# A two-layer recurrent kernel on one core: the small part of the output projection run as two half-height products side by side

## The chip, the cores and the metric

The kernel runs on one core of one Trainium2 chip. The metric is the device time of one execution in microseconds, the median over the executions that were timed. Lower is better.

## The reference: what is computed

The input `x` has 128 rows (batch), 128 time steps and 512 features; `cond` has 128 rows of 512. Two layers are added to `x` one after the other. The first is a state-space layer: a convolution over time and a projection give a gate pair `B_t`, `C_t` of 64 numbers each, `u = x @ Ws` gives 64 numbers, a state decays and accumulates, and its read-out `y` (64 numbers a step) is projected back to 512 features by `Wo`. The second is a plain recurrent layer with a 512 by 512 matrix. Cut to what matters:

```python
def step(state, inputs):
    u_t, b_t, c_t = inputs
    state = decay * state + dt * b_t * u_t
    return (state, c_t * state)
...
return y @ Wo + bo
...
def step(h, xw_t):
    h_next = jnp.tanh(h @ Wh + xw_t)
    return (h_next, h_next)
...
x = x + _L0_cond_ref(x, cond_1024[:, None, :], ...)
x = x + _L1_cond_ref(x, cond_1024, ...)
```

## The kernel before, in words

**Precision by splitting.** Most products are taken in the float32r type. An operand is split into a high part (the value rounded to float32r) and a low part (the rest), and a product is made of several: high by high, high by low, low by high. Names end in `_hi` and `_lo` for the parts. `y_hl` holds both parts of `y` in one tile of 128 rows: the low part of the 64 numbers in rows 0 to 63 (`0:N`), the high part in rows 64 to 127 (`N:P`). `wo_hi` and `wo_lo` hold the scaled `Wo` twice, once in each half of the rows, so that one product of `wo_hi` (128 rows) with `y_hl` sums high and low `y` at once.

**Stages.** The first 311 us or so hold the convolution, the transposes and the projection (lines 705 to 716 and 768 to 789). Then a loop over 32 groups of four time steps runs (`steps`, lines 791 to 818 for TensorE, with a body of the same shape on ScalarE, VectorE and GpSimd). Two groups are written out ahead, a hardware loop covers the middle, and the last ones are written out behind. In group g the recurrence of the second layer runs its four steps, and in the gaps the first layer of group g+1 is computed.

**One step on TensorE** is: `z_first` of the next step (8 products of 512 columns, lines 746 and 747), four transposes of the new `h` (line 801), `z_second` (4 products, line 753) and `z_recur` (12 products, lines 761, 762, 765). Beside that, step 0 holds `u_second` (4 products, line 728), step 3 holds `u_first` (4 products, line 722) ahead of its `z_second`, and step 2 holds `wo_product` (lines 731 to 738) between `z_second` and `z_recur`: for each of four chunks c of 128 output features, `wo_hi` by `y_hl` (line 736) and `wo_lo` by `y_hl` (line 737) are summed in one PSUM bank.

**The chain from wo_product to the next group.** When a chunk's bank is done (`wo_done`), VectorE adds it to `x` (`x1_sum`, line 591, chunks 0 and 1 right after line 633, then line 636, then chunks 2 and 3). ScalarE rounds the sum to the high part `x1_hi` (`x1_copy`, line 433), GpSimd subtracts for the low part `x1_lo` (`x1_rest`, line 354), chunk by chunk in order. TensorE's `z_first(0)` at the end of step 2 wants `x1_hi`; its `z_second(0)` in step 3 waits until all four chunks of `x1_lo` are there (line 812). In the last group with such a product the instruction `u_first` is missing in step 3, so `z_second(0)` comes at once behind the transposes.

**The high part of y** is made in step 2 on ScalarE (`y_copy`, line 428, between the tanh of line 460 and the copy `hT_hi` of line 464); VectorE subtracts for the low part (`y_rest`, line 579). In every engine the order of instructions is written out by hand, and engines meet by counting semaphores. The product for group 0 is made ahead of the loop, two chunks at m = 17 and two at m = 21 (lines 777 to 781), with the copy of `y` at m = 15.

In the profile the digits of a tile's name are left out: `x1_f`, `x1_hi`, `x1_lo` read as `x_f`, `x_hi`, `x_lo`, and a PSUM bank is `bank`.

Of the kernel before, what the change touches and what calls it, by code (L numbers as in the profile page):

```python
# [6 lines left out]
F32R = mybir.dt.float32r  # L7
# [4 lines left out]
BATCH = 128  # L12
TIME = 128
D = 512
N = 64
P = 128
KC = D // P
# [4 lines left out]
G = 4  # L22
# [13 lines left out]
def wait(engine, sem, value):  # L36

    if not isinstance(value, int) or value > 0:
        engine.wait_ge(sem, value)


def build(nc, x_rev, x_dtb, hankel, h0_t, vectors, Wp, Ws, Wo, Wx, Wh, b, out):
# [5 lines left out]
    ctx = ExitStack()  # L48
    with ctx:
        def sb(stack, name, shape, dt=F32):  # L50
            return stack.enter_context(nc.sbuf_tensor(name, shape, dt))

        def sem(name):
            return ctx.enter_context(nc.semaphore(name))
# [44 lines left out]
        wo_lo = sb(ctx, "wo_lo", [P, D], F32R)  # L99
        wo_hi = sb(ctx, "wo_hi", [P, D], F32R)  # L100
        soft_slots = sb(ctx, "soft_slots", [P, SOFT_SLOTS, 512])


        with ExitStack() as first:
# [11 lines left out]
        y_f = sb(ctx, "y_f", [P, G * BATCH])  # L116
        y_hl = sb(ctx, "y_hl", [P, G * BATCH], F32R)
# [16 lines left out]
        def soft(q):  # L134

            return soft_slots[:, q if isinstance(q, int) and q < EARLY else 0]
# [5 lines left out]
        def rows_of_c(par):  # L142
            return rows_of_b(1 - par)
# [10 lines left out]
        def conv_room(c, m):  # L154

            if c % 2 == 0:
                return conv[:, bass.ts(m, PER_BANK)]
            return conv[:, :, bass.ts(m, PER_BANK)]

        def conv_out(c, m):  # L160

            if c % 2 == 0:
                return CONV[m % 4][:].rearrange("p (d l) -> p d l", d=PER_BANK)
            return CONV[m % 4][:].rearrange("p (d l) -> p l d", d=PER_BANK)
# [5 lines left out]
        def turn_bank(c, m):  # L170
            return LAST_TURN[m % 3] if c == LAST else TURN[m % 2]
# [4 lines left out]
        def turned_slot(c, m):  # L176
            return turned[:, (BANKS * c + m) % SLOTS]
# [37 lines left out]
        s_ready = sem("s_ready")  # L215
        y_ready = sem("y_ready")
        yhi_ready = sem("yhi_ready")
        ylo_ready = sem("ylo_ready")
        wo_done = sem("wo_done")
        x1_ready = sem("x1_ready")  # L220
# [150 lines left out]
        @block.scalar  # L371
        def _(act):

            nc.scalar.preload_act_table_set("natural_log_exp_and_others")
            act.wait_ge(rate_step, 1)
            nc.scalar.activation(rates_e[:], rates[:, 0:2], ACT.Exp).then_inc(rate_act, 1)
            act.wait_ge(rate_act, 1)
            nc.scalar.activation(rates[:, 2:4], rates_e[:], ACT.Ln, bias=1.0).then_inc(rate_act, 1)

            def copy_conv(c, m):  # L380

                act.wait_ge(conv_done, BANKS * c + m + 1)
                nc.scalar.copy(conv_room(c, m), conv_out(c, m))\
                  .then_inc(conv_copied_act, 1)

            def copy_turned(c, m):

                act.wait_ge(turn_done, BANKS * c + m + 1)
                out = turned_slot(c, m) if c == LAST else turned_hl[:, 0, m % 2]
                nc.scalar.activation(out, turn_bank(c, m)[:], ACT.Identity, bias=conv_b[:, c:c + 1])\  # L390
                  .then_inc(turn_copied, 1)

            act.wait_ge(vec_loaded, DMA)
            for m in range(0, BANKS, 2):
                copy_conv(0, m)
            for c in range(KC - 1):
                for m in range(BANKS):
                    copy_turned(c, m)
                    copy_conv(c + 1, m)
            nc.scalar.preload_act_table_set("exp_and_others")  # L400

            def u_copy(g):
                act.wait_ge(u_done, g + 1)
                nc.scalar.copy(u_lo[:], UB[N:P, :]).then_inc(ulo_ready, 1)

            def tanh_c(g, par):

                wait(act, y_ready, g)
                cols = bass.ds(g * (G * BATCH), G * BATCH)
                nc.scalar.activation(c_f[N:P, :], bc[rows_of_c(par), cols], ACT.Tanh).then_inc(c_ready, 1)  # L410

            def soft_exp(q):
                act.wait_ge(abs_ready, 2 * q + 2)
                nc.scalar.activation(soft(q), soft(q), ACT.Exp, scale=-1.0).then_inc(exp_ready, 1)

            def soft_ln(q):
                act.wait_ge(exp_ready, q + 1)
                nc.scalar.activation(soft(q), soft(q), ACT.Ln, bias=1.0).then_inc(ln_ready, 1)

            def split_x(g, par):  # L420
                act.wait_ge(x_loaded[par], DMA * ((g - par) // 2 + 1) if isinstance(g, int) else (g - par) * (DMA // 2) + DMA)
                wait(act, u_done, g)
                nc.scalar.copy(x_hi[:], x_f[par][:]).then_inc(xhi_ready, 1)

            def y_copy(g):
                act.wait_ge(y_ready, g + 1)
                wait(act, wo_done, KC * g)
                nc.scalar.copy(y_hl[N:P, :], y_f[N:P, :]).then_inc(yhi_ready, 1)

            def x1_copy(g, par, chunks=range(KC)):  # L430
                for c in chunks:
                    act.wait_ge(x1_ready, KC * g + c + 1)
                    nc.scalar.copy(x1_hi[:, c], x1_f[par][:, c]).then_inc(x1hi_ready, 1)  # L433

            for m in range(BANKS):
                copy_turned(LAST, m)
                if m == 3:

                    act.wait_ge(proj_added, BANKS * LAST + 1)
                    c_0 = bc[rows_of_c(0), 0:G * BATCH]  # L440
                    nc.scalar.activation(c_0, c_0, ACT.Tanh).then_inc(c_ready, 1)
                    nc.scalar.preload_act_table_set("natural_log_exp_and_others")
                if m in (5, 7):
                    soft_exp((m - 5) // 2)
                if m in (6, 8):
                    soft_ln((m - 6) // 2)
                if m == 8:
                    nc.scalar.preload_act_table_set("exp_and_others")
                if m == 9:
                    u_copy(0)  # L450
                if m == 15:
                    y_copy(0)
                if m in (20, 21, 24, 25):
                    x1_copy(0, 0, ((20, 21, 24, 25).index(m),))

            def steps(g, par, first, last, q):
                for s in range(G):
                    t = g * G + s
                    act.wait_ge(zsum_ready, t + 1)
                    nc.scalar.activation(h_f[:], z_f[:], ACT.Tanh).then_inc(h_ready, 1)  # L460
                    if s == 2 and not last:
                        y_copy(g + 1)
                    act.wait_ge(ht_done, t + 1)
                    nc.scalar.copy(hT_hi[:], HB[s % 2][:].rearrange("p (c b) -> p c b", c=KC)).then_inc(hthi_ready, 1)  # L464
                    if last:
                        continue
                    if q is not None and par == 0 and s == 3:

                        nc.scalar.preload_act_table_set("natural_log_exp_and_others")
                        soft_ln(q)  # L470
                        nc.scalar.preload_act_table_set("exp_and_others")
                    if s == 0:
                        u_copy(g + 1)
                        tanh_c(g + 1, 1 - par)
                        if q is not None and par == 0:
                            soft_exp(q)
                    if s == 2:
                        x1_copy(g + 1, 1 - par)
                    if s == 1 and not (isinstance(g, int) and g == GROUPS - 2):
                        split_x(g + 2, par)  # L480

            groups(act, steps)

        @block.vector
# [169 lines left out]
        def _(pe):  # L654
# [76 lines left out]
            def wo_product(g, banks, chunks):  # L731

                pe.wait_ge(yhi_ready, g + 1)
                pe.wait_ge(ylo_ready, g + 1)
                for c in chunks:
                    nc.tensor.matmul(banks[c][:], wo_hi[:, bass.ts(c, P)], y_hl[:], start=True, stop=False)  # L736
                    nc.tensor.matmul(banks[c][:], wo_lo[:, bass.ts(c, P)], y_hl[:], start=False, stop=True)\  # L737
                      .then_inc(wo_done, 1)

            def z_first(s, after=None):  # L740

# [122 lines left out]
```

## Time and profile before

| what | value |
|---|---|
| median of 3 executions | 1185.26 us (1185.19 to 1185.41) |
| the profiled execution | 1186.63 us, of which the span of the trace 1184.5 us |
| granted clock of TensorE in the profiled execution | 0.999 of full speed |
| TensorE busy with products (PE) | 1158.7 us, 98% of the span, 5984 instructions |
| VectorE (DVE), ScalarE (ACT), GpSimd (POOL) busy | 681.2, 562.3, 332.7 us |
| share of the last-ending chain on TensorE | 95% |

A profile row gives the start or the count, the line of the kernel, the engine, the operation, the tile that is written and those that are read. PEld is TensorE's loading of the stationary operand, which runs beside the product before it. The duration of a product is modelled and includes a latency that the next product overlaps: the distance between starts tells the cost of one in a stream.

### The profile page before, as it was taken

The numbers are of one execution on the slowest core, as the hardware profiler recorded it, in microseconds if no ns is written. First come the engines' busy times: TensorE is split into PE (matmuls) and PEld (weight loads), VectorE is DVE, ScalarE is ACT, GpSimd is POOL, SyncE is SP. The second block draws the span as 40 slices with busy tenths as digits, with TensorE's granted clock in tenths as the row PEclk, the third lists the DMA queues.
The fourth block names the chain that finished last, engine by engine and source line by source line (L and its number), as shares of the span: only waits on it lengthen the run. The fifth ranks groups of instructions, "written<-read, shape, count | busy, mean of one in ns | idle before, by whom it ended". The sixth has DMA issues, their size and how long they took to land.

```text
span 1184.5 us, 15976 instructions
## 1 busy us (share of the span) xinstructions
PE 1158.7 (98%) x5984; PEld 968.5 (82%) x5984; DVE 681.2 (58%) x1078; ACT 562.3 (47%) x816; POOL 332.7 (28%) x180
## 2 busy tenths in 40 slices
PE   6799999999999999999999999999999999999997
PEld 5799999985788888888888888888888888888886
DVE  1367677667555555555655656555555555555553
ACT  2255666575354544535354445454454545453431
POOL 0000005021233444433333333344433333333340
PEclk9999999999999999999999999999999999999999
DMA  9988877730122222222222222222223222222202
GB/s 350 385 290 285 254 259 247 243 99 20 61 72 72 72 71 71 92 91 91 80 71 71 71 71 71 71 71 71 87 91 91 86 71 71 71 71 71 72 36 71
DMA packets 81424, 137.97 MB, mean 116 GB/s; under 512 B 3888, under 2 KB 39728, under 8 KB 81392
## 3 DMA queue, kind: packets, MB, share of 16 engines
q1 hardware_dynamic: 81392, 137.51, 35.4%
q8 instruction: 24, 0.39, 0.1%
q14 instruction: 8, 0.07, 0.0%
HBM read 103.95 MB, written 33.55 MB: 116 GB/s over the span
## 4 chain that ended last, share of the span: by engine, by line
PE 95%; DMA 3%; DVE 1%; POOL 0%; issue 0%; ACT 0%; SPq 0%; POOLq 0%; DVEq 0%
PE bank L753 10%; PE bank L761 10%; PE bank L762 10%; PE bank L747 10%; PE bank L765 10%; PE bank L746 10%; PE bank L672 9%; PE bank L687 5%; PE bank L801 5%; DMA ring<-x_rev 3%; PE bank L722 3%; PE bank L728 3%; PE bank L736 2%; PE bank L737 2%; PE bank L701 2%; PE bank L703 2%
## 5 line engine op out<-in xcount | busy, mean ns | idle before, releaser
L354 POOL TENSOR_TENSOR x_lo<-x_f,x_hi 128x512 fp32r<-128x512 f32 x128 | 161.7, 1290 | 588.2 <-ACT x_hi L433 588.1
L460 ACT ACTIVATE h_f<-z_f 128x512 f32<-128x512 f32 x128 | 80.9, 632 | 296.7 <-DVE z_f L624 296.7
L761 PE MATMUL bank<-wh_hi,hT_hi 128*128 128x512 f32 x512 | 200.8, 392 | 0.0
L762 PE MATMUL bank<-wh_lo,hT_hi 128*128 128x512 f32 x512 | 199.9, 390 | 0.0
L747 PE MATMUL bank<-wx_lo,x_hi 128*128 128x512 f32 x512 | 199.7, 390 | 0.0
L746 PE MATMUL bank<-wx_hi,x_hi 128*128 128x512 f32 x512 | 199.6, 390 | 0.0
L633 DVE TENSOR_TENSOR hT_lo<-bank,hT_hi 128x512 fp32r<-128x512 f32 x128 | 88.6, 692 | 186.8 <-ACT hT_hi L464 186.8
L624 DVE TENSOR_TENSOR z_f<-bank,b_rows 128x512 f32<-128x512 f32 x128 | 88.6, 692 | 132.2 <-PE bank L765 129.2
L672 PE MATMUL bank<-ring 128*128 128x128 f32 x1024 | 138.6, 280 | 16.9 <-DMA ring<-x_rev 16.9
L348 POOL TENSOR_TENSOR x_lo<-x_f,x_hi 128x2048 fp32r<-128x2048 f32 x32 | 147.6, 4612 | 1.5 <-PE bank L672 1.4
L672 PEld LDWEIGHTS bank<-ring 128*128 128x128 f32 x1024 | 129.5, 194 | 19.3 <-DMA ring<-x_rev 12.7
L753 PE MATMUL bank<-wx_hi,x_lo 128*128 128x512 f32 x512 | 144.7, 404 | 0.4 <-POOL x_lo L354 0.4
L765 PE MATMUL bank<-wh_hi,hT_lo 128*128 128x512 f32 x512 | 137.0, 389 | 0.0
L464 ACT CAST hT_hi<-bank 128x512 fp32r<-128x512 f32 x128 | 75.1, 587 | 94.5 <-PE bank L801 94.5
L761 PEld LDWEIGHTS bank<-wh_hi,hT_hi 128*128 128x128 f32 x512 | 96.1, 188 | 26.2 <-ACT hT_hi L464 6.1
L433 ACT CAST x_hi<-x_f 128x512 fp32r<-128x512 f32 x128 | 79.6, 622 | 74.3 <-DVE x_f L591 71.8
L765 PEld LDWEIGHTS bank<-wh_hi,hT_lo 128*128 128x128 f32 x512 | 96.1, 188 | 20.4
L746 PEld LDWEIGHTS bank<-wx_hi,x_hi 128*128 128x128 f32 x512 | 96.1, 188 | 20.2 <-issue 0.2
L747 PEld LDWEIGHTS bank<-wx_lo,x_hi 128*128 128x128 f32 x512 | 96.1, 188 | 20.2 <-issue 0.2
L762 PEld LDWEIGHTS bank<-wh_lo,hT_hi 128*128 128x128 f32 x512 | 96.2, 188 | 19.7 <-issue 0.2
L753 PEld LDWEIGHTS bank<-wx_hi,x_lo 128*128 128x128 f32 x512 | 91.2, 188 | 17.2 <-POOL x_lo L354 0.6
L516 DVE SCALAR_TENSOR_TENSOR turned_hl<-bank,vec,turned_hl 128x512 fp32r<-128x512 f32 x96 | 72.1, 751 | 50.9 <-ACT turned_hl L390 50.9
(77 smaller groups left out, 1595.0 us busy)
## 6 DMA issues: line engine op xcount, KB each, us to landing
ring<-hankel SPq DMA_DIRECT2D x64, 512.0 KB, 4.5
ring<-x_rev SPq DMA_DIRECT2D x64, 512.0 KB, 5.5
x_f<-x_dtb SPq DMA_DIRECT2D x32, 1024.0 KB, 8.2
out<-x_f SPq DMA_DIRECT2D x31, 1024.0 KB, 5.4
wx_f<-Wx SPq DMA_DIRECT2D x1, 1024.0 KB, 8.0
wh_f<-Wh SPq DMA_DIRECT2D x1, 1024.0 KB, 7.9
out<-x_f SPq DMA_DIRECT2D x4, 256.0 KB, 2.2
wp_f<-Wp SPq DMA_DIRECT2D x1, 384.0 KB, 9.8
```

Source lines behind the costliest of these rows:

```text
L348: nc.gpsimd.tensor_tensor(x_lo[:], x_f[par][:], f(x_hi[:]), ALU.subtract).then_inc(xlo_ready, 1)
L354: nc.gpsimd.tensor_tensor(x1_lo[:, c], x1_f[par][:, c], f(x1_hi[:, c]), ALU.subtract)\
L460: nc.scalar.activation(h_f[:], z_f[:], ACT.Tanh).then_inc(h_ready, 1)
L624: nc.vector.tensor_tensor(z_f[:], ZB[s % 2][:], b_rows[:], ALU.add).then_inc(zsum_ready, 1)
L633: nc.vector.tensor_tensor(hT_lo[:], turned_h, f(hT_hi[:]), ALU.subtract).then_inc(htlo_ready, 1)
L672: mm = nc.tensor.matmul(CONV[m % 4][:, bass.ts(d % PER_BANK, TIME)], x_part(slot)[:, d % CH], t_part(slot)[:, d % CH // 2, :, d % 2], star ...
L746: nc.tensor.matmul(z, x1_hi[:, k, s], wx_hi[:, k], start=(k == 0), stop=False)
L747: nc.tensor.matmul(z, x1_hi[:, k, s], wx_lo[:, k], start=False, stop=False)
L753: mm = nc.tensor.matmul(z, x1_lo[:, k, s], wx_hi[:, k], start=False, stop=stop and k == KC - 1)
L761: nc.tensor.matmul(z, hT_hi[:, k], wh_hi[:, k], start=False, stop=False)
L762: nc.tensor.matmul(z, hT_hi[:, k], wh_lo[:, k], start=False, stop=False)
L765: mm = nc.tensor.matmul(z, hT_lo[:, k], wh_hi[:, k], start=False, stop=stop and k == KC - 1)
```

## The change

Chunks are taken in pairs. For each pair the two products with `wo_hi` stay as they were. The two products with `wo_lo` now read 64 rows each: chunk c-1 takes rows 0 to 63 of `wo_lo` and of a new tile `y_hi`, chunk c takes rows 64 to 127 of `wo_lo` and of `y_hl`, where the high part of `y` lies. So the low part of `y` by the low part of `Wo` is no longer part of the sum, and the two products use different rows of the array. Since the high part of `y` was held in rows 64 to 127 alone, ScalarE makes a second copy of it in rows 0 to 63 (`y_copy_low`, 64x512), ahead of the loop behind `y_copy(0)`, and in step 2 behind the copy `hT_hi`. A new semaphore `yhi_copied` is waited for by TensorE before each pair.

```diff
+        y_hi = sb(ctx, "y_hi", [N, G * BATCH], F32R)
...
+        yhi_copied = sem("yhi_copied")
...
+            def y_copy_low(g):
+                wait(act, wo_done, KC * g)
+                nc.scalar.copy(y_hi[:], y_f[N:P, :]).then_inc(yhi_copied, 1)
...
                 if m == 15:
                     y_copy(0)
+                    y_copy_low(0)
...
                     nc.scalar.copy(hT_hi[:], HB[s % 2][:].rearrange("p (c b) -> p c b", c=KC)).then_inc(hthi_ready, 1)
                     if last:
                         continue
+                    if s == 2:
+                        y_copy_low(g + 1)
...
                 for c in chunks:
                     nc.tensor.matmul(banks[c][:], wo_hi[:, bass.ts(c, P)], y_hl[:], start=True, stop=False)
-                    nc.tensor.matmul(banks[c][:], wo_lo[:, bass.ts(c, P)], y_hl[:], start=False, stop=True)\
-                      .then_inc(wo_done, 1)
+                    if c % 2 == 1:
+                        pe.wait_ge(yhi_copied, g + 1)
+                        nc.tensor.matmul(banks[c - 1][:], wo_lo[0:N, bass.ts(c - 1, P)], y_hi[:], start=False, stop=True)\
+                          .then_inc(wo_done, 1)
+                        nc.tensor.matmul(banks[c][:], wo_lo[N:P, bass.ts(c, P)], y_hl[N:P, :], start=False, stop=True)\
+                          .then_inc(wo_done, 1)
```

On TensorE in step 2, between `z_second` and `z_recur`, before (line 736 is the product with `wo_hi`, 737 that with `wo_lo`):

```order
L753 MATMUL bank<-wx_hi,x_lo 128x512 x4
L736 MATMUL bank<-y_hl,wo_hi 128x512 [waits ylo_ready,yhi_ready]
L737 MATMUL bank<-y_hl,wo_lo 128x512
L736 MATMUL bank<-y_hl,wo_hi 128x512
L737 MATMUL bank<-y_hl,wo_lo 128x512
L736 MATMUL bank<-y_hl,wo_hi 128x512
L737 MATMUL bank<-y_hl,wo_lo 128x512
L736 MATMUL bank<-y_hl,wo_hi 128x512
L737 MATMUL bank<-y_hl,wo_lo 128x512
L759 REGISTER_ALU
L761 MATMUL bank<-wh_hi,hT_hi 128x512 [waits hthi_ready]
```

The same place in the changed kernel (line 766 was 753, 745 is the product with `wo_hi`, 748 and 750 are the two of 64 rows, 774 was 761):

```order
L766 MATMUL bank<-wx_hi,x_lo 128x512 x4
L745 MATMUL bank<-y_hl,wo_hi 128x512 [waits ylo_ready,yhi_ready]
L745 MATMUL bank<-y_hl,wo_hi 128x512
L748 MATMUL bank<-y_hi,wo_lo 128x512 [waits yhi_copied]
L750 MATMUL bank<-y_hl,wo_lo 128x512
L745 MATMUL bank<-y_hl,wo_hi 128x512 x2
L748 MATMUL bank<-y_hi,wo_lo 128x512 [waits yhi_copied]
L750 MATMUL bank<-y_hl,wo_lo 128x512
L772 REGISTER_ALU
L774 MATMUL bank<-wh_hi,hT_hi 128x512 [waits hthi_ready]
```

The number of products is the same; the first product with `wo_lo` stands third instead of second, behind a wait for ScalarE, and chunk 0 is done with it.

On ScalarE in step 2 of a group inside the loop, the changed kernel (430 was 428, 471 was 464, 439 was 433):

```order
L39 REGISTER_ALU [waits y_ready]
L430 CAST y_hl<-y_f 64x512 [waits wo_done]
L471 CAST hT_hi<-bank 128x512 [waits ht_done]
L434 CAST y_hi<-y_f 64x512 [waits wo_done]
L438 REGISTER_ALU
L439 CAST x_hi<-x_f 128x512 [waits x1_ready]
```

The new copy (line 434) stands between `hT_hi` and the copies of `x1`; before, these followed each other with nothing between. The orders on VectorE, GpSimd and SyncE are the same as before.

## Rows read from the trace of the kernel before

**Rows 1.** The page: busy time by engine, and the last-ending chain by engine.
```profile
PE 1158.7 (98%) x5984; PEld 968.5 (82%) x5984; DVE 681.2 (58%) x1078; ACT 562.3 (47%) x816; POOL 332.7 (28%) x180
PE 95%; DMA 3%; DVE 1%; POOL 0%; issue 0%; ACT 0%; SPq 0%; POOLq 0%; DVEq 0%
```
**Rows 2.** Timeline of PE, one group: start us, duration us, engine, line, operation, tiles, count.
```profile
709.40 0.60 PE L801 MATMUL bank<-ident,h_f 128*128 128x128 f32 x4
709.75 1.18 PE L753 MATMUL bank<-wx_hi,x_lo 128*128 128x512 f32 x4
710.77 0.40 PE L736 MATMUL bank<-y_hl,wo_hi 128*128 128x512 f32 x1
711.01 0.39 PE L737 MATMUL bank<-y_hl,wo_lo 128*128 128x512 f32 x1
...
712.60 0.39 PE L761 MATMUL bank<-wh_hi,hT_hi 128*128 128x512 f32 x1
...
717.13 0.60 PE L801 MATMUL bank<-ident,h_f 128*128 128x128 f32 x4
717.49 1.18 PE L722 MATMUL bank<-x_hi,ws_hl 128*128 128x512 f32 x4
718.51 1.08 PE L753 MATMUL bank<-wx_hi,x_lo 128*128 128x512 f32 x4
```
**Rows 3.** Line 737 on PE: durations in ns, least, median, most.
```profile
L737 PE MATMUL bank<-y_hl,wo_lo x128: 389/389/402, 283.3 to 1150.2; 128*128 128x512 f32 x128
```
**Rows 4.** Timeline of DVE, same group; in brackets the idle time before and its end.
```profile
711.51 1.41 DVE L591 SCALAR_TENSOR_TENSOR x_f<-bank,vec,x_f 128x512 f32<-128x512 f32 x2 [0.16 <-PE bank L737]
```
**Rows 5.** Timeline of ACT, steps 1 and 2 of the same group.
```profile
704.09 0.59 ACT L464 CAST hT_hi<-bank 128x512 fp32r<-128x512 f32 x1 [0.90 <-PE bank L801]
704.58 1.91 ACT L423 CAST x_hi<-x_f 128x2048 fp32r<-128x2048 f32 x1
708.51 0.63 ACT L460 ACTIVATE h_f<-z_f 128x512 f32<-128x512 f32 x1 [2.02 <-DVE z_f L624]
709.16 0.61 ACT L428 CAST y_hl<-y_f 64x512 fp32r<-64x512 f32 x1
710.03 0.59 ACT L464 CAST hT_hi<-bank 128x512 fp32r<-128x512 f32 x1 [0.26 <-PE bank L801]
712.29 1.28 ACT L433 CAST x_hi<-x_f 128x512 fp32r<-128x512 f32 x2 [1.67 <-DVE x_f L591]
```
**Rows 6.** Timeline of PEld: a load that waited for ACT, and the loads of transposes.
```profile
704.73 0.19 PEld L761 LDWEIGHTS bank<-wh_hi,hT_hi 128*128 128x128 f32 x1 [0.18 <-ACT hT_hi L464]
716.92 0.57 PEld L801 LDWEIGHTS bank<-ident,h_f 128*128 128x128 f32 x4
717.46 0.77 PEld L722 LDWEIGHTS bank<-x_hi,ws_hl 128*128 128x128 f32 x4
```
**Rows 7.** Timeline of POOL, the same group and one 109 us earlier.
```profile
712.99 5.06 POOL L354 TENSOR_TENSOR x_lo<-x_f,x_hi 128x512 fp32r<-128x512 f32 x4 [17.73 <-ACT x_hi L433]
718.00 4.62 POOL L348 TENSOR_TENSOR x_lo<-x_f,x_hi 128x2048 fp32r<-128x2048 f32 x1
603.52 5.05 POOL L354 TENSOR_TENSOR x_lo<-x_f,x_hi 128x512 fp32r<-128x512 f32 x4 [17.73 <-ACT x_hi L433]
```
**Rows 8.** Timeline of PE, the group of the last row of group 7.
```profile
601.54 0.39 PE L737 MATMUL bank<-y_hl,wo_lo 128*128 128x512 f32 x1
609.04 0.62 PE L753 MATMUL bank<-wx_hi,x_lo 128*128 128x512 f32 x2
```
**Rows 9.** Timelines of POOL, PEld and PE in the last group that holds such a product.
```profile
1150.86 5.04 POOL L354 TENSOR_TENSOR x_lo<-x_f,x_hi 128x512 fp32r<-128x512 f32 x4 [17.73 <-ACT x_hi L433]
1155.95 0.19 PEld L753 LDWEIGHTS bank<-wx_hi,x_lo 128*128 128x128 f32 x1 [0.59 <-POOL x_lo L354]
1155.96 1.20 PE L753 MATMUL bank<-wx_hi,x_lo 128*128 128x512 f32 x4 [0.35 <-POOL x_lo L354]
1156.99 0.39 PE L761 MATMUL bank<-wh_hi,hT_hi 128*128 128x512 f32 x1
```
**Rows 10.** Who waited for whom: total us, times, longest.
```profile
PEld bank L753 <- POOL x_lo L354: 0.6, 1, 0.6
```

## The prediction
> **What bounds the kernel now.** I read the page first: TensorE is busy 98% of the span and carries 95% of the last-ending chain [rows 1]. So whatever TensorE no longer does shortens the kernel, as long as nothing that it waits for comes in its place. Next the timeline of TensorE in one group [rows 2]: the eight products of `wo_product` begin at 710.77 and `z_recur` follows at 712.60, so from the first `wo_lo` product (711.01) there are seven distances in 1.59 us, 0.227 each, although one product lasts 0.389 by its row [rows 3]. The stream has no holes there. Third I looked for what stands just behind TensorE. `z_second(0)` of step 3 starts at 718.51 [rows 2] and wants all of `x1_lo`. GpSimd starts on it at 712.99 and needs 5.06, until 718.05 [rows 7]. It is not waited for now, except in the last group, where TensorE comes earlier [rows 9, 10]. But it is close, and it hangs on `wo_product` by a chain of fixed steps: `wo_lo` product of chunk 0 at 711.01 [rows 2], VectorE's sum at 711.51 [rows 4], ScalarE's copy at 712.29 [rows 5], GpSimd at 712.99, end 718.05 [rows 7]. That is 7.04 us from the start of that one product to the last of `x1_lo`.
>
> **How much room that chain has.** In the last group GpSimd ends at 1150.86 + 5.04 = 1155.90, the waiting load starts at 1155.95, and the first product behind the four of `z_second` starts at 1156.99 [rows 9]. Four products back (0.907) is 1156.08: TensorE is back in its stream 0.18 us after GpSimd's end. In the group shown it could be so at 718.05 + 0.18 = 718.23, and gets there at 718.51. The room is 0.28 us. The group at 603 us gives 609.04 - (603.52 + 5.05) - 0.18 = 0.29 [rows 7, 8].
>
> **The change part by part.**
>
> *TensorE's own work.* Four products with `wo_lo` become two pairs. If a pair costs what one product does, 2 x 0.227 = 0.454 us per group go. The rows show no product of 64 rows, so a pair lies between 0.227 (side by side) and 0.454 (one after the other); I take it near side by side, plus one load. The stationary loads of transposes follow each other after 0.11 us (four from 716.92, the last ones until 717.46) [rows 6], so the second half of the first pair can start 0.11 late when both loads sit behind the wait; in the second pair they run beside the product before.
>
> *Going from full to half height and back,* four times a group. The nearest row is the change from transposes to products: from 709.40, four transposes at 0.11 and four products at 0.227 make 1.35 of the 1.37 us until 710.77 [rows 2], so that change cost 0.02 us. The other end: a product cannot start until the one before it has ended, 0.389 - 0.227 = 0.162 [rows 2, 3], and if its load must wait as well, 0.27. I take 0.02, the row of a real change of the array's use, and keep the rest for a rival. A gain by the change of height is excluded, since it adds no overlap that the pair doesn't already have.
>
> *The second copy of y* on ScalarE. It stands behind `hT_hi`, which starts at 710.03. In step 1 the cast behind `hT_hi` starts 0.49 after it (704.09, 704.58) [rows 5]; the cast of 64x512 takes 0.61. So it ends at 710.03 + 0.49 + 0.61 = 711.13. A load that waits for ScalarE starts 0.05 after (704.68 to 704.73) [rows 6], so 711.18, and its product 0.11 later, 711.29. Without the wait that product would start at 711.01 + 0.227 = 711.24. The wait costs 0.05. Upper end: if the copy starts 0.65 after, as `y_hl` behind the tanh does (708.51, 709.16) [rows 5], it costs 0.21; lower end 0. Behind this copy ScalarE has nothing until 712.29 [rows 5], so it holds up nothing else there.
>
> *Chunk 0 is done later.* Its `wo_lo` product moves from 711.01 to 711.29, plus 0.02 for the change of height: 0.30 later. VectorE, ScalarE and GpSimd follow by their fixed steps, so GpSimd ends 0.30 later. The room was 0.28. **So TensorE's saving turns into a wait for GpSimd**: its own work would bring it to `z_second(0)` at 718.51 - 0.454 + 0.05 + 0.11 + 4 x 0.02 = 718.30, GpSimd lets it go on at 718.23 + 0.30 = 718.53.
>
> *The sum.* Thirty groups: 0.30 - 0.28 = +0.02 each, +0.6. The last group waited for GpSimd already and takes the whole delay, +0.30. The product ahead of the loop has no such chain at its heels and keeps its saving, -0.454 + 4 x 0.02, about -0.4. Together +0.5 us: on the profiled execution 1186.63 + 0.5 = 1187.1, and since that one lies 1.4 above the median of the runs, 1185.26 + 0.5 = **1185.8** against that median. With the wait at its ends (0 and 0.21) the thirty groups give -0.9 and +5.4 and the last one 0.25 and 0.46, so this case by itself holds 1184.2 to 1190.7.
>
> **The rivals.**
>
> *The change of height empties the array (slower).* Each of the four changes then costs 0.16 to 0.27. TensorE's own work becomes 4 x 0.16 - 0.454 = +0.19 to 4 x 0.27 - 0.454 = +0.63 a group, more than GpSimd's chain (0.16 - 0.05 = 0.11 later at the low end) and with the wait for `y` inside the first change. Times 31 and the one ahead: +6.1 to +20.2, so 1191.4 to 1205.5, middle 1198. It decides from about 0.13 a change, where four make the 0.454 that is saved and the 0.08 a group that 0.2% of the time is. For it: nothing in the trace shows a product that uses part of the rows, so nothing shows the change to be cheap; against it: the change from transposes to products costs next to nothing [rows 2]. The Trainium skill says in TensorEngine Tiling (Array Packing), section Key Properties, that changing the tiling mode, and not just the tile, drains the TensorE. By that rule the sum would be this rival's and not mine; no run here shows it yet, and the page gives no price.
>
> *The halves don't run side by side.* A pair takes 0.454 and nothing is saved. Without dear changes of height TensorE then loses the wait and little else, 0.05 to 0.13 a group: +1.6 to +4, 1187 to 1189. Speaking for it: nothing in the rows shows two products at once.
>
> *GpSimd's chain is not in the way (faster).* If the four subtractions or a step ahead of them get shorter by the 0.23 that TensorE would wait, the products decide: -0.21 to -0.45 a group, -7 to -14, 1171 to 1178. For it: GpSimd does the same number of elements in one instruction in 4.62 instead of 5.06 [rows 7], so 0.4 of its time is between pieces. Against it: the four took 5.04 to 5.06 in each group shown [rows 7, 9], and nothing in the change touches them.
>
> **How the numbers follow.** A measurement of this kernel can tell about 0.2% from no change, 2.4 us. The forecast gets 0.42 (0.35 within that, 0.05 slower by the dear end of the wait, 0.02 faster). The emptied array gets 0.39, all slower. The halves in a row get 0.08, half within 0.2% and half slower. GpSimd out of the way gets 0.09, faster. 0.02 is left for a delay that I don't see, slower. That is 0.11 faster, 0.39 same, 0.50 slower; the likeliest single case is still the forecast. The range from 1183.5 to 1203 leaves out the fast rival (0.09), the top of the emptied array (0.05), halves in a row with dear changes (0.03) and the rest (0.02).
>
> **What would show it.** Right: in the table of waits `z_second`'s load waits for GpSimd's `x1_lo` in all of the 31 groups instead of one, 0.2 to 0.4 us each, TensorE's busy share falls, the pair's second product starts at most 0.11 behind the first, and the load of the first waits about 0.2 for ScalarE's copy. The change of height shows in the distance from the second product of a pair to the next one: 0.23 to 0.25 supports me, 0.39 or more the emptied array. Wrong: no waits for GpSimd, with the group's period (27.37 us: GpSimd's two starts, 712.99 and 603.52, are four groups apart [rows 7]) down by 0.2 or more, or up by as much.

## The result and the profile after

The changed kernel takes 1198.09 us (median of 5, 1197.11 to 1198.69) where the kernel before takes 1185.26 (1185.12 to 1185.41) beside it: 1.0104 times as long, 95% interval 1.009 to 1.0118. That lies inside the range, but it is not the forecast, 1185.8, nor within what that case held by itself (1184.2 to 1190.7). It is where the rival of the emptied array lay, whose middle was 1198. The granted clock of TensorE was 1.000 in the profiled execution (0.999 before), so the clock is not the cause.

The page of the changed kernel, busy time by engine and the chain by engine, against [rows 1]:

```profile
span 1195.0 us, 16008 instructions
PE 1169.4 (98%) x5984; PEld 950.4 (80%) x5984; DVE 681.0 (57%) x1078; ACT 578.6 (48%) x848; POOL 332.7 (28%) x180
PE 94%; DMA 3%; DVE 1%; SPq 0%; POOL 0%; issue 0%; ACT 0%; POOLq 0%; DVEq 0%
```

TensorE still carries the chain and is still 98% busy; it has the same number of instructions and 10.7 us more busy time. ScalarE has 32 instructions more (the copies, 0.6 us each). Nothing says yet where the time sits. The timeline of TensorE in one group does, columns as in [rows 2] (line 745 is the product with `wo_hi`, 748 and 750 are the halves of a pair, 774 and 775 the first products of `z_recur`):

```profile
604.07 0.63 PE L745 MATMUL bank<-y_hl,wo_hi 128*128 128x512 f32 x2
604.63 0.50 PE L748 MATMUL bank<-y_hi,wo_lo 64*128 64x512 f32 x1
604.64 0.50 PE L750 MATMUL bank<-y_hl,wo_lo 64*128 64x512 f32 x1
605.07 0.73 PE L745 MATMUL bank<-y_hl,wo_hi 128*128 128x512 f32 x2
605.73 0.50 PE L748 MATMUL bank<-y_hi,wo_lo 64*128 64x512 f32 x1
605.73 0.49 PE L750 MATMUL bank<-y_hl,wo_lo 64*128 64x512 f32 x1
606.16 0.50 PE L774 MATMUL bank<-wh_hi,hT_hi 128*128 128x512 f32 x1
606.50 0.40 PE L775 MATMUL bank<-wh_lo,hT_hi 128*128 128x512 f32 x1
```

The two halves of a pair start within 0.01 us. The work from the first product with `wo_hi` to the second of `z_recur` takes 606.50 - 604.07 = 2.43; before it took 712.60 + 0.227 - 710.77 = 2.06 [rows 2]. That is 0.37 more a group. GpSimd's starts give the same: from 606.73 (shown further down) to the start four groups later it is 110.93 us, 27.73 a group, where it was 27.37.

```profile
717.66 5.05 POOL L356 TENSOR_TENSOR x_lo<-x_f,x_hi 128x512 fp32r<-128x512 f32 x4 [18.11 <-ACT x_hi L439]
```

Over the 31 groups that hold such a product this is 11.5 us, of the 12.8 (10.7 to 14.0 by the interval) that were measured. The streaming in it (four products and two pairs at the price of six products) would be 0.454 shorter than before, so 0.37 + 0.454, some 0.83, was added: 0.21 for each of the four changes between 128 and 64 rows.

What a change consists of is to be seen in the loads of the stationary operand (PEld) in the same group:

```profile
603.92 0.35 PEld L745 LDWEIGHTS bank<-y_hl,wo_hi 128*128 128x128 f32 x2
604.63 0.18 PEld L748 LDWEIGHTS bank<-y_hi,wo_lo 64*128 64x128 f32 x1 [0.37 <-ACT y_hi L434]
604.63 0.18 PEld L750 LDWEIGHTS bank<-y_hl,wo_lo 64*128 64x128 f32 x1
605.07 0.30 PEld L745 LDWEIGHTS bank<-y_hl,wo_hi 128*128 128x128 f32 x2 [0.25 <-issue]
605.73 0.18 PEld L748 LDWEIGHTS bank<-y_hi,wo_lo 64*128 64x128 f32 x1 [0.36 <-issue]
```

In a stream of one height the load runs beside the product before it; in the kernel before, one starts 0.23 ahead of its own product:

```profile
711.01 0.19 PEld L736 LDWEIGHTS bank<-y_hl,wo_hi 128*128 128x128 f32 x1
```

```profile
711.24 0.39 PE L736 MATMUL bank<-y_hl,wo_hi 128*128 128x512 f32 x1
```

In the changed kernel each load of the other height starts together with its own product, not earlier: at 604.63, 605.07, 605.73. The modelled duration of the products behind a change is 0.50 instead of 0.39: the 0.11 is the load that stands in the open. And it starts late: the last product with `wo_hi` (the second of the two at 605.07) started at 605.40, and the load of the pair behind it at 605.73, 0.33 later, where in a stream already the next product would have started after 0.227.

```profile
605.40 0.40 PE L745 MATMUL bank<-y_hl,wo_hi 128*128 128x512 f32 x1
```

So a change costs some 0.10 until the array takes the next load and some 0.11 for that load. The Trainium skill, TensorEngine Tiling (Array Packing), section Key Properties, says that changing the tiling mode drains the TensorE; the trace agrees in that no load runs ahead across a change, with 0.21 us a change as the price the page doesn't give. What exactly the load waits for inside the array no row shows: it starts 0.07 before the modelled end of the last product.

The table of waits names a different cause for the first change of a group, and it is wrong there:

```profile
PEld bank L748 <- issue: 12.0, 33, 0.4
PEld bank L748 <- ACT y_hi L434: 11.4, 31, 0.4
PEld bank L745 <- issue: 10.0, 32, 2.3
PEld bank L774 <- issue: 7.8, 32, 0.2
PEld bank L766 <- POOL x_lo L356: 0.6, 1, 0.6
```

11.4 us are put down to ScalarE's copy of `y`, which is about the whole loss. But the copy, on ScalarE's timeline in the same group, had ended 0.19 before the load began (603.82 + 0.62 = 604.44 against 604.63):

```profile
603.34 0.59 ACT L471 CAST hT_hi<-bank 128x512 fp32r<-128x512 f32 x1 [0.26 <-PE bank L814]
603.82 0.62 ACT L434 CAST y_hi<-y_f 64x512 fp32r<-64x512 f32 x1
```

and the second pair, which waits for nothing, has the same idle time of 0.36. The last row of the waits answers to [rows 10]: GpSimd was waited for once, as before. Its row against [rows 7], and the product that wants it:

```profile
606.73 5.06 POOL L356 TENSOR_TENSOR x_lo<-x_f,x_hi 128x512 fp32r<-128x512 f32 x4 [18.11 <-ACT x_hi L439]
```

```profile
612.19 1.08 PE L766 MATMUL bank<-wx_hi,x_lo 128*128 128x512 f32 x4
```

It ends at 611.79, TensorE arrives at 612.19: with the 0.18 of the prediction the room is 0.22. Counted from the first product with `wo_hi`, GpSimd's start comes 0.44 later than before (606.73 - 604.07 = 2.66 against 712.99 - 710.77 = 2.22) and TensorE's arrival 0.38 later (8.12 against 7.74). So the chain was delayed a little more than TensorE; it used 0.06 of the room of 0.28 and did not become the bound.

### The profile page after: what moved, and what is told of

Its sections match the earlier page's. It is cut to its first block, busy times and chain, and to the rows that moved or that the text cites. A ratio compares the mean times of both kernels' runs of the same rounds, so it can differ in the third digit from the quotient of the medians.

```text
span 1195.0 us, 16008 instructions
## 1 busy us (share of the span) xinstructions
PE 1169.4 (98%) x5984; PEld 950.4 (80%) x5984; DVE 681.0 (57%) x1078; ACT 578.6 (48%) x848; POOL 332.7 (28%) x180
## 4 chain that ended last, share of the span: by engine, by line
PE 94%; DMA 3%; DVE 1%; SPq 0%; POOL 0%; issue 0%; ACT 0%; POOLq 0%; DVEq 0%
PE bank L774 10%; PE bank L766 10%; PE bank L775 10%; PE bank L760 10%; PE bank L778 10%; PE bank L759 10%; PE bank L681 8%; PE bank L696 5%; PE bank L814 5%; DMA ring<-x_rev 3%; PE bank L745 3%; PE bank L737 2%; PE bank L731 2%; PE bank L748 2%; PE bank L710 2%; PE bank L712 2%
## 5 line engine op out<-in xcount | busy, mean ns | idle before, releaser
L774 PE MATMUL bank<-wh_hi,hT_hi 128*128 128x512 f32 x512 | 204.0, 398 | 0.0
L681 PE MATMUL bank<-ring 128*128 128x128 f32 x1024 | 137.6, 278 | 16.7 <-DMA ring<-x_rev 16.6
```

The costliest lines, as they stand in the source:

```text
L681: mm = nc.tensor.matmul(CONV[m % 4][:, bass.ts(d % PER_BANK, TIME)], x_part(slot)[:, d % CH], t_part(slot)[:, d % CH // 2, :, d % 2], star ...
L774: nc.tensor.matmul(z, hT_hi[:, k], wh_hi[:, k], start=False, stop=False)
```

## The experiments

Theories: the **empty array** (each change of height costs 0.21, a pair costs one product); the **halves in a row** (a pair takes 0.44 because the two halves don't overlap, a change only 0.10: the rows above fit that as well, since they show starts and not ends); the **wait** (ScalarE's copy, its semaphore, chunk 0's third place). Ratios are to the kernel before on the same chip.

**full_height: the order, the copy and the wait, without halves.**

```diff
-                        nc.tensor.matmul(banks[c - 1][:], wo_lo[0:N, bass.ts(c - 1, P)], y_hi[:], start=False, stop=True)\
+                        nc.tensor.matmul(banks[c - 1][:], wo_lo[:, bass.ts(c - 1, P)], y_hl[:], start=False, stop=True)\
...
-                        nc.tensor.matmul(banks[c][:], wo_lo[N:P, bass.ts(c, P)], y_hl[N:P, :], start=False, stop=True)\
+                        nc.tensor.matmul(banks[c][:], wo_lo[:, bass.ts(c, P)], y_hl[:], start=False, stop=True)\
```

> The changed kernel with its order, its second copy of y and its wait kept, but both products with wo_lo again over all 128 rows of y_hl. If the changes of height cost the time (empty array, or a load that can't run ahead), it is all gone and TensorE loses only the wait, about 0.05 us a group: 1186 to 1187 us. If the wait for the copy, the third place of chunk 0's product or ScalarE's longer list cost the time, it stays near 1198.

1188.16 us, ratio 1.0027 (1.0017 to 1.0037). Ten of the 13 us are gone with the halves, so the wait is not the main cause. Its true price can be read here, on TensorE's timeline:

```profile
710.64 0.62 PE L745 MATMUL bank<-y_hl,wo_hi 128*128 128x512 f32 x2
711.10 0.45 PE L748 MATMUL bank<-y_hl,wo_lo 128*128 128x512 f32 x1
711.38 0.40 PE L750 MATMUL bank<-y_hl,wo_lo 128*128 128x512 f32 x1
711.62 0.62 PE L745 MATMUL bank<-y_hl,wo_hi 128*128 128x512 f32 x2
```

711.10 to 711.38 is 0.28 instead of 0.227: 0.05, as the prediction had it. This group is a short one; the same distance goes up to 0.31 in others. Four groups by GpSimd's starts take 109.84 us, 27.46 each instead of 27.37:

```profile
603.30 5.04 POOL L356 TENSOR_TENSOR x_lo<-x_f,x_hi 128x512 fp32r<-128x512 f32 x4 [17.84 <-ACT x_hi L439]
713.14 5.04 POOL L356 TENSOR_TENSOR x_lo<-x_f,x_hi 128x512 fp32r<-128x512 f32 x4 [17.83 <-ACT x_hi L439]
```

That is 0.09 a group, 2.8 us over 31, inside the 2.0 to 4.4 that the ratio says; the wait is 0.05 to 0.08 of it. The profiled span is only 1.5 longer than that of the kernel before, because in that trace the first product with `wo_hi` comes 1.28 later (283.00 against 281.72), ahead of the loop.

**half_each: every product with wo_lo alone on half the rows, in the order of the kernel before.**

```diff
-                    nc.tensor.matmul(banks[c][:], wo_lo[:, bass.ts(c, P)], y_hl[:], start=False, stop=True)\
+                    nc.tensor.matmul(banks[c][:], wo_lo[N:P, bass.ts(c, P)], y_hl[N:P, :], start=False, stop=True)\
```

> The kernel before in its own order, only each product with wo_lo reads rows 64 to 127 alone (the low part of y by wo_lo is left out): eight changes of height a group, no pair, no copy, no wait. Empty array, side by side (a pair costs one product plus two changes of 0.21): each product with wo_lo costs 0.227 + 0.41, the group 8 x 0.21 = 1.65 more, 1185 + 53 = 1238 us. Halves one after the other (a pair costs 0.44 in itself and a change only 0.10): 8 x 0.10 = 0.8 more a group, 1211. Wait or copy as the cause: 1185.

1240.34 us, ratio 1.0455 (1.0438 to 1.0473). No copy, no wait, and the largest loss: 55.4 us, 55.4 / 32 / 8 = 0.216 a change. Part of that is the clock. In this trace the granted clock fell to half (1.2 of 2.4 GHz) twice inside the loop, each time behind the eight products of `wo_product`, and the two groups took 30.6 us each (419.10 to 449.70 here) where the others took 28.97 (683.16 to 712.13):

```profile
452.00:454.00 2.00, 2.00 (x6) 1.52 (x6) 0.00 (x0) 0.32 (x1) 2.00 (x3) 0.50 0.00 0
```

```profile
419.10 5.01 POOL L354 TENSOR_TENSOR x_lo<-x_f,x_hi 128x512 fp32r<-128x512 f32 x4 [19.37 <-ACT x_hi L433]
449.70 5.01 POOL L354 TENSOR_TENSOR x_lo<-x_f,x_hi 128x512 fp32r<-128x512 f32 x4 [21.02 <-ACT x_hi L433]
...
683.16 5.04 POOL L354 TENSOR_TENSOR x_lo<-x_f,x_hi 128x512 fp32r<-128x512 f32 x4 [19.34 <-ACT x_hi L433]
712.13 5.04 POOL L354 TENSOR_TENSOR x_lo<-x_f,x_hi 128x512 fp32r<-128x512 f32 x4 [19.36 <-ACT x_hi L433]
```

(The first row is of 452 to 454 us: length, busy time of each engine with its instructions, then the granted clock, 0.50.) In a group at full clock it is 28.97 - 27.37 = 1.60, 0.20 a change. TensorE's timeline:

```profile
710.06 0.49 PE L737 MATMUL bank<-y_hl,wo_lo 64*128 64x512 f32 x1
710.48 0.50 PE L736 MATMUL bank<-y_hl,wo_hi 128*128 128x512 f32 x1
710.91 0.50 PE L737 MATMUL bank<-y_hl,wo_lo 64*128 64x512 f32 x1
711.34 0.50 PE L736 MATMUL bank<-y_hl,wo_hi 128*128 128x512 f32 x1
```

One product of 64 rows between two changes takes 0.43, like one of 128 rows between two changes, and like a whole pair in the changed kernel (604.63 to 605.07). So the pair's second half came free, and the 0.43 is one product and one change. The halves in a row are out.

**same_half: the changed kernel's order with both halves in the same rows.** The diff is to the kernel before.

```diff
                 for c in chunks:
                     nc.tensor.matmul(banks[c][:], wo_hi[:, bass.ts(c, P)], y_hl[:], start=True, stop=False)
-                    nc.tensor.matmul(banks[c][:], wo_lo[:, bass.ts(c, P)], y_hl[:], start=False, stop=True)\
-                      .then_inc(wo_done, 1)
+                    if c % 2 == 1:
+                        for d in (c - 1, c):
+                            nc.tensor.matmul(banks[d][:], wo_lo[N:P, bass.ts(d, P)], y_hl[N:P, :], start=False, stop=True)\
+                              .then_inc(wo_done, 1)
```

> The order of the changed kernel, but both products of a pair read rows 64 to 127, so they can't stand side by side; no second copy of y and no wait (the low part of y by wo_lo is left out, as in the change). Side by side in the changed kernel: here each pair takes one product more, 2 x 0.227 x 32 = 14.5 us above it, 1212 to 1213. Halves one after the other in the changed kernel already: the same 1198, or 1 to 2 less for the wait. Wait or copy as the cause: 1185 to 1187.

1211.53 us, ratio 1.0221 (1.0204 to 1.0238). As expected of halves that do overlap in the changed kernel: 13.4 us above it for 64 products of 0.227 (14.5). Against the kernel before nothing is saved and four changes are paid: 26.6 / 32 / 4 = 0.21 each.

**one_trip: two changes a group instead of four.** The diff is to the changed kernel; the product ahead of the loop keeps its four.

```diff
-                for c in chunks:
-                    nc.tensor.matmul(banks[c][:], wo_hi[:, bass.ts(c, P)], y_hl[:], start=True, stop=False)
-                    if c % 2 == 1:
...
+                first = chunks[0]
+                nc.tensor.matmul(banks[first][:], wo_hi[:, bass.ts(first, P)], y_hl[:], start=True, stop=False)
+                pe.wait_ge(yhi_copied, g + 1)
+                for c in chunks[1::2]:
+                    mm = nc.tensor.matmul(banks[c - 1][:], wo_lo[0:N, bass.ts(c - 1, P)], y_hi[:],
+                                          start=c - 1 != first, stop=c - 1 == first)
...
+                    nc.tensor.matmul(banks[c][:], wo_lo[N:P, bass.ts(c, P)], y_hl[N:P, :], start=True, stop=False)
+                for c in chunks[1:]:
+                    nc.tensor.matmul(banks[c][:], wo_hi[:, bass.ts(c, P)], y_hl[:], start=False, stop=True)\
+                      .then_inc(wo_done, 1)
```

> The two pairs moved together: chunk 0's product with wo_hi, both pairs, then the other three products with wo_hi; two changes of height a group in the loop instead of four, with the copy on ScalarE and its wait kept (the first product, ahead of the loop, still has four). Empty array at 0.21 a change: 0.41 a group less, of which the earlier need for the copy gives back up to 0.15: 1185 to 1190 us. Halves one after the other with 0.10 a change: 0.2 a group less, 1191 to 1193. Wait as the cause: above 1198, since the copy is wanted 0.2 us earlier.

1188.4 us, ratio 1.0033 (1.0023 to 1.0043): 9.7 us less than the changed kernel for two changes a group fewer. The copy is now wanted earlier, and from the first product to the first pair it is 0.41, where 0.33 would be 0.227 and the emptying; so the wait shows with 0.08. Two changes fewer at 0.21 less this wait, over 31 groups, are 10.5:

```profile
710.49 0.39 PE L745 MATMUL bank<-y_hl,wo_hi 128*128 128x512 f32 x1
710.90 0.50 PE L748 MATMUL bank<-y_hi,wo_lo 64*128 64x512 f32 x1
```

**pairs_last: also two changes, but chunk 0 done late.** The diff is to the changed kernel, whose copy stays.

```diff
                 for c in chunks:
                     nc.tensor.matmul(banks[c][:], wo_hi[:, bass.ts(c, P)], y_hl[:], start=True, stop=False)
-                    if c % 2 == 1:
-                        pe.wait_ge(yhi_copied, g + 1)
-                        nc.tensor.matmul(banks[c - 1][:], wo_lo[0:N, bass.ts(c - 1, P)], y_hi[:], start=False, stop=True)\
-                          .then_inc(wo_done, 1)
-                        nc.tensor.matmul(banks[c][:], wo_lo[N:P, bass.ts(c, P)], y_hl[N:P, :], start=False, stop=True)\
-                          .then_inc(wo_done, 1)
+                pe.wait_ge(yhi_copied, g + 1)
+                for c in chunks[1::2]:
+                    nc.tensor.matmul(banks[c - 1][:], wo_lo[0:N, bass.ts(c - 1, P)], y_hi[:], start=False, stop=True)\
+                      .then_inc(wo_done, 1)
+                    nc.tensor.matmul(banks[c][:], wo_lo[N:P, bass.ts(c, P)], y_hl[N:P, :], start=False, stop=True)\
+                      .then_inc(wo_done, 1)
```

> The changed kernel with both pairs behind all four products with wo_hi: two changes of height a group in the loop, and no wait for the copy, since it is done by then; but chunk 0 is done later than in any other order. TensorE's own work is then 0.04 less a group than before the change. Empty array alone, without the chain through GpSimd: 1184 us. With that chain: VectorE's sum of chunk 0 comes 0.88 later than before the change, GpSimd ends 0.88 later, the room of 0.28 is used up, 0.6 a group: 1202 to 1205, with a wait for GpSimd's x1_lo in every group.

1204.28 us, ratio 1.0161 (1.0145 to 1.0176). TensorE has no more to do than in one_trip, and the kernel is 16 us slower: the chain through GpSimd, which the forecast rested on, is real. The waits, and one group on GpSimd and TensorE:

```profile
PEld bank L766 <- POOL x_lo L356: 24.2, 31, 1.5
```

```profile
721.19 5.07 POOL L356 TENSOR_TENSOR x_lo<-x_f,x_hi 128x512 fp32r<-128x512 f32 x4 [18.37 <-ACT x_hi L439]
```

```profile
726.31 1.19 PE L766 MATMUL bank<-wx_hi,x_lo 128*128 128x512 f32 x4 [0.34 <-POOL x_lo L356]
```

GpSimd ends at 726.26 and TensorE goes on 0.05 later, in 31 groups instead of one.

**no_lo: no product with wo_lo at all.**

```diff
-                    nc.tensor.matmul(banks[c][:], wo_hi[:, bass.ts(c, P)], y_hl[:], start=True, stop=False)
-                    nc.tensor.matmul(banks[c][:], wo_lo[:, bass.ts(c, P)], y_hl[:], start=False, stop=True)\
+                    nc.tensor.matmul(banks[c][:], wo_hi[:, bass.ts(c, P)], y_hl[:], start=True, stop=True)\
```

> The kernel before without the four products with wo_lo (the whole small part of wo is left out of the sum); no change of height, no copy. TensorE's own work falls by 4 x 0.227 = 0.91 us a group. If the chain through VectorE, ScalarE and GpSimd stands behind it as the prediction read it, that chain starts only 0.14 earlier (VectorE is busy until then), TensorE waits about 0.5 for the low part of x1 in every group, and a group gains 0.42: 1171 to 1173 us. If the chain is not in the way, the whole 0.91 is gained: 1156.

1168.41 us, ratio 0.9858 (0.9843 to 0.9873). TensorE lost 29 us of work and the kernel only 16.7: the other 12 became waiting for GpSimd, again in 31 groups (the row counts idle time of the loads, a part of which the products ahead cover):

```profile
PEld bank L752 <- POOL x_lo L354: 17.6, 31, 1.3
```

The forecast was about 3 us too high. It let VectorE's sum of chunk 0 start 0.14 earlier than in the kernel before, held up by the instruction ahead of it. Counted from the first product with `wo_hi` the sum began 0.50 later here (701.38 - 700.88) and 0.74 later before (711.51 - 710.77), so it came 0.24 earlier, only 0.62 after the start of the instruction ahead, which lasts 0.69. The 0.10 between them makes 3.1 us over 31 groups:

```profile
700.88 1.08 PE L736 MATMUL bank<-y_hl,wo_hi 128*128 128x512 f32 x4
```

```profile
700.76 0.69 DVE L633 TENSOR_TENSOR hT_lo<-bank,hT_hi 128x512 fp32r<-128x512 f32 x1 [0.16 <-ACT hT_hi L464]
701.38 1.41 DVE L591 SCALAR_TENSOR_TENSOR x_f<-bank,vec,x_f 128x512 f32<-128x512 f32 x2
```

**one_trip_pool: two changes and no wait.** The order on TensorE is that of one_trip. GpSimd, idle at that time, makes the second copy by subtracting a tile of zeros from `y_f`. Of the diff, which is to the kernel before, the copy alone:

```diff
+                pool.wait_ge(y_ready, g + 1)
+                wait(pool, wo_done, KC * g)
+                nc.gpsimd.tensor_tensor(y_hi, y_f[N:P, :], zeros, ALU.subtract).then_inc(yhi_copied, 1)
```

> As one_trip, but GpSimd makes the second copy of y from y_f, as soon as VectorE has y, instead of ScalarE behind hT_hi. If what one_trip has over the kernel before is the wait for that copy (0.08 a group in its trace), it goes: 0.33 instead of 0.41 from the first product to the first pair, the eight products take 1.79 instead of 1.83 before the change, 1183 to 1185 us, at most 0.2% faster than before. If two changes of height cost more than the 0.454 that the pairs save, it stays at 1187 or more.

1184.81 us, ratio 1.0000 (0.9991 to 1.0009), no different from the kernel before and 3.6 us less than one_trip. TensorE's timeline:

```profile
709.03 0.40 PE L744 MATMUL bank<-y_hl,wo_hi 128*128 128x512 f32 x1
709.36 0.49 PE L747 MATMUL bank<-y_hi,wo_lo 64*128 64x512 f32 x1
...
709.70 0.39 PE L747 MATMUL bank<-y_hi,wo_lo 64*128 64x512 f32 x1
...
710.02 0.98 PE L753 MATMUL bank<-y_hl,wo_hi 128*128 128x512 f32 x3
```

0.33 to the first pair, as reckoned. The second pair follows after 0.34 with a duration of 0.39: within one height the loads run ahead again, and only the way in and out is paid, 0.33 - 0.227 + 0.11 in, the same out. Two changes at 0.21 are 0.42, the pairs save 0.454, and the 0.03 left are 1 us. This is the best that any order tried here gave: a draw. No version that keeps high `y` by `wo_lo` beat the kernel before.

## Why the prediction was right or wrong

- **Where the time fell.** The range held the result because it took in a rival; the forecast's own case missed it by 7 us. Both signs that the prediction named for this were met: from the second product of a pair to the next one it is 0.43 (0.39 or more was to be the emptied array), and the group's period rose by 0.37 with GpSimd waited for once.
- **The change of height: wrong, and it alone decides.** The prediction took 0.02, the row of the change between transposes and products, "the row of a real change of the array's use", and kept 0.16 to 0.27 for a rival. Measured: 0.20 to 0.21, four ways (0.21 in the changed kernel, 0.20 with eight changes at full clock, 0.21 with four and no pair, 0.21 by the rows of one_trip_pool with two). The nearest row was not the nearest case: transposes and products both use all 128 rows. The rival's own sum with 0.21, 4 x 0.21 - 0.454 = 0.39 a group over 32, is 12.3 us; 12.8 were measured. Its condition also held: it decides from 0.13 a change. That its middle, 1198, met the time to 0.1 us is luck: neither of its ends is what happens. 0.16 was to be the wait for the end of the product before and 0.27 that and the load; the load shows with its 0.11, but the wait ahead of it is 0.10.
- **Half of the rows, side by side: right.** A pair costs what one half costs (half_each), and without the overlap it is 13.4 us more (same_half). The halves in a row fell.
- **The second copy and its wait: right, 0.05 to 0.08 a group where nothing covers it** (full_height). In the changed kernel the first change of height covers it, as the rival said.
- **The chain through VectorE, ScalarE and GpSimd: right, but not reached.** pairs_last gave the 0.88 of delay less 0.28 of room that the prediction's steps give, no_lo the wait in every group. In the changed kernel TensorE comes later than GpSimd, so the forecast of 31 waits did not come true. The rival let the chain be delayed less than TensorE; it was delayed by 0.44 against 0.38, since chunk 0's product waits for the first change and its load stands in the open as well, and the room covered the difference.
- **The saving ahead of the loop**, 0.4 by the forecast, turned into a loss of about 0.2 by the traces: for the later two chunks it is 1.58 us instead of 1.49 from the first product with `wo_hi` (288.43, before 289.50) to the first product behind the next transposes (290.01, before 290.99), and about as much for the first two.
- **The chances.** The likeliest case was to have been no change at 0.42 against 0.39 for the emptied array. The slower side had 0.50 in all and the range reached to 1203, so the sum of the cases stood better than the choice among them, which was wrong.

## What to carry to other kernels

Products on half of the array's rows do run two at a time, but each change between full and half height cost 0.21 us here, nearly a whole product of 512 columns; so a pair must not be bought alone. Put all products of one height together, reckon two changes for each stay, and look whether what is done later by that order feeds a chain that has no room. When a row of waits names a releaser, look when that engine had ended: the 11.4 us put down to ScalarE's copy belonged to the change of height.

## What the runs showed of the hardware that was not expected

- The load of the stationary operand runs ahead within a stay at half height as it does at full height (second pair after 0.34, duration 0.39), but in no row shown across the change (durations of 0.49 to 0.50 behind it).
- Two VectorE instructions in a row can start 0.62 apart though the first lasts 0.69 (no_lo), so a start reckoned from the end of the instruction ahead comes out late (0.10 in no_lo).
- In half_each the granted clock fell from 2.4 to 1.2 GHz in stretches at 420 to 424 and 450 to 454 us (0.57 and 0.62 over these four us), right behind eight products that started 0.43 apart. In the changed kernel, with two pairs and four changes a group, it stayed at full speed.
